# Three edits in the routed-expert tail of a fused vision kernel: when the experts' weights are asked for, what the token store waits for, and how 256 scatter slots are shared

## Chip, cores and metric

The kernel runs on one core of a Trainium2 chip. The metric is the device time of one execution in microseconds (us); of several runs the median counts. Five engines matter: TensorE (PE; its weight loads are shown as PEld), VectorE (DVE), ScalarE (ACT), GpSimd (POOL) and SyncE (SP), which only issues DMA transfers. ACT and POOL issue transfers as well. All of them run on the core's 16 DMA engines.

## The reference, cut to what matters

The input is `x` of shape (2, 64, 256, 256). Two blocks follow each other: a shift convolution with a recurrent layer over the 65,536 tokens, then a linear attention with a mixture of experts. The change touches only the last part, the experts. With 2 batches, 64 channels, 32 experts, 8 tokens for each expert and 256 hidden units it is:

```
probs = softmax(logits, axis=1)                      # over the tokens, for each expert
vals, idx = top_k(probs.transpose(0, 2, 1), K)       # 8 best tokens of each expert
gathered = take_along_axis(x, flat_idx[:, :, None], axis=1)
pooled = einsum('bked,bke->bed', gathered, topv)
h = gelu(einsum('ebd,edh->ebh', [pooled, 1], weight1))
out = einsum('ebh,eho->ebo', [h, 1], weight2)
outputs = zeros.at[batch, flat_idx].add(out * topv)  # scattered back to the tokens
x = x + outputs
```

So each batch has 32 x 8 = 256 slots, a slot being one (expert, token) pair. A token that several experts chose appears in several slots.

## The kernel before

Both batches lie beside each other on the 128 partitions, 64 channels each. The kernel is a series of blocks of engine programs. All up to the last stream the 65,536 tokens through the engines in tiles of 512 tokens and blocks of 2048, software-pipelined by an order written out by hand; that part is not touched. By its end each of 32 blocks of tokens has left its 8 best logits for each expert (`cand`), their places (`best_at`) and its sums of exponentials (`ses`), and the output without the experts' part is already in `out`.

The last block, the tail, is one serial program in which the engines wait for each other by semaphores. DVE counts its instructions on the semaphore `dv`; the names `DV_MAX`, `DV_TOK` and so on are the counts at which others may go on. In order:

1. SP merges the candidates of both halves with six transfers into `c2`, `i2`, `se2` (L1689 to L1691). ACT meanwhile asks for the experts' weights (L1711 to L1716), about 4.2 MB, loads a table (L1717) and then waits for `DV_MAX`.
2. DVE takes the maximum (`t8`, L1833), its places, and in eight steps the token numbers `tokf`, cast to `toki` (L1842). ACT takes two exponentials (L1719, L1720), and DVE scales them to the probabilities `prob` (L1847). That is `DV_TOK`.
3. SP stores `toki`, `tokf` and `prob` to DRAM (L1693 to L1695), waits for all three, and reads them back in the layouts that are needed: `toki2` (one slot for each partition, 4-byte pieces) on the semaphore `back`; `tokc` (likewise), and as broadcasts to all partitions `tokr`, `tokq`, `pr`, on `back2` (L1697 to L1703). The trace calls `toki2` token_of_slot and `tokq` token_by_channel.
4. From `toki2` DVE makes row addresses (L1855 to L1860), and POOL gathers the chosen tokens from DRAM with eight indirect transfers (L1744). DVE waits for all seven transfers of `back2` and finds which slots hold the same token (L1866, L1867), PE counts the later repeats (L1766), and DVE makes the scatter's addresses `word` and `byte_of_slot` (L1871 to L1875); all but the last slot of a token get an address past the end, and the transfer is skipped.
5. PE turns the gathered tokens (L1771), DVE copies them to `xg` (L1878), and the norm follows in short steps on PE, ACT and DVE; DVE multiplies by `pr` (L1882) and pools (L1883). PE waits for `w_loaded` and runs the experts: L1787 and L1790 with `w1` (64 weight loads of 128 columns), L1794 and L1798 with `w2` (128 of 64 columns). More short steps give `fin` (L1903), the new value of each slot's token.
6. `DV_FIN` releases the scatter. Slots 72 to 255 (`SHARED` = 184) are written by SP for the first batch and by ACT for the second, one transfer of 64 words for each slot, its address read from `byte_of_slot` into a register (L1676 to L1680). Slots 0 to 71 are written by POOL with one indirect transfer for both batches (L1751).

Of the kernel before, what the change touches and what calls it, by code (L numbers as in the profile page):

```python
# [7 lines left out]
F32 = mybir.dt.float32  # L8
# [3 lines left out]
ACT = mybir.ActivationFunctionType  # L12
# [3 lines left out]
B, C, H, W = 2, 64, 256, 256  # L16
P = B * C
# [11 lines left out]
E, K, HID = 32, 8, 256  # L29
# [38 lines left out]
def build_program(nc, x, conv_k, ffn_w, ffn_v, gamma, beta, q_w, q_b, kv_w, kv_b, proj_w, proj_b,  # L68
                  gate_w, gate_b, w1, w2, const, out, debug=None):
# [3 lines left out]
    with stack:  # L73
        def sb(name, shape, dt=F32, where=stack):
            return where.enter_context(nc.sbuf_tensor(name, shape, dt))
# [14 lines left out]
        tokf_d = dram("token_f_scratch", (B * E * K,))  # L90
        prob_d = dram("prob_scratch", (B * E * K,))
# [41 lines left out]
        with ExitStack() as ph:  # L133
# [7 lines left out]
            @blk.gpsimd  # L141
            def _(pool):
                for t in (w_rows, src["v"], src["q"], src["p"], src["g"], src["kv0"], src["kv1"]):
                    pool.memset(t[:, :], 0.0).then_inc(zeroed, 1)
                pool.memset(eps_c, EPS_C).then_inc(zeroed, 1)
                pool.memset(eps_t, EPS_T).then_inc(zeroed, 1)
                pool.memset(eps_z, EPS_Z).then_inc(zeroed, 1)
                pool.memset(ones[:, :], 1.0).then_inc(zeroed, 1)
                pool.memset(pair_mean[:, :], 0.0).then_inc(zeroed, 1)
                for b in range(B):  # L150
                    d = slice(b * C, (b + 1) * C)
                    for col, vec in ((qb, q_b), (pb, proj_b), (gam, gamma), (bet, beta)):
                        pool.dma_start(col[d, :], vec.rearrange("(c o) -> c o", o=1)).then_inc(vectors_loaded, 16)
                for r in range(4):
                    pool.dma_start(gb[r * E:(r + 1) * E, :], gate_b.rearrange("(c o) -> c o", o=1)).then_inc(vectors_loaded, 16)
# [62 lines left out]
        with ExitStack() as ph:  # L218
# [24 lines left out]
            S = lambda n: sem(n, ph)  # L243
# [416 lines left out]
        with ExitStack() as ph:  # L660
# [14 lines left out]
            S = lambda n: sem(n, ph)  # L675
# [262 lines left out]
        with ExitStack() as ph:  # L938
# [4 lines left out]
            S = lambda n: sem(n, ph)  # L943
# [87 lines left out]
        with ExitStack() as ph:  # L1031
# [15 lines left out]
            S = lambda n: sem(n, ph)  # L1047
# [543 lines left out]
        with ExitStack() as ph:  # L1591
            NC = NBLK * K
            w1_sb = sb("w1_sb", [P, E // 2, HID], F32, ph)
            w1b_sb = sb("w1b_sb", [E, HID], F32, ph)
            w2_sb = sb("w2_sb", [P, 2, E, C], F32, ph)
            w2b_sb = sb("w2b_sb", [E, C], F32, ph)
            cidx = sb("cidx", [P, NC], F32, ph)
            c2 = sb("c2", [64, 2 * NC], F32, ph)
# [53 lines left out]
            gp = S("tail_pool")  # L1652
            w_loaded = S("expert_weights_loaded")
            scat0, scat1 = S("columns_out_batch0"), S("columns_out_batch1")
            back2, rep, turned_back = S("broadcasts_back"), S("repeats_counted"), S("tokens_turned")
            blk = ph.enter_context(nc.Block())
            ONE = dict(allow_slow_non_contiguous=True)

            SHARED = 184
            AT_ONCE = 8
            SKIP = float(2 ** 28)
            PAST_END = float(4 * B * C * N)
# [18 lines left out]
            @blk.sync  # L1683
            def _(sp):

                sp.wait_ge(placed, 1)
                for j in range(2):
                    rows = slice(j * 64, (j + 1) * 64)
                    sp.dma_start(c2[:, j * NC:(j + 1) * NC], cand[rows, :]).then_inc(merged, 16)  # L1689
                    sp.dma_start(i2[:, j * NC:(j + 1) * NC], cidx[rows, :]).then_inc(merged, 16)  # L1690
                    sp.dma_start(se2[:, j * NBLK:(j + 1) * NBLK], ses[rows, :]).then_inc(merged, 16)  # L1691
                sp.wait_ge(dv, DV_TOK)
                sp.dma_start(tok_d.rearrange("(p k) -> p k", k=K), toki[:, :]).then_inc(out_tok, 16)  # L1693
                sp.dma_start(tokf_d.rearrange("(p k) -> p k", k=K), tokf[:, :]).then_inc(out_tok, 16)
                sp.dma_start(prob_d.rearrange("(p k) -> p k", k=K), prob[:, :]).then_inc(out_tok, 16)  # L1695
                sp.wait_ge(out_tok, 48)
                sp.dma_start(toki2[:, :, :].rearrange("p b j -> p (b j)"), tok_d.rearrange("(n p) -> p n", p=P), **ONE).then_inc(back, 16)  # L1697
                sp.dma_start(tokc[:, :, :].rearrange("p b j -> p (b j)"), tokf_d.rearrange("(n p) -> p n", p=P), **ONE).then_inc(back2, 16)
                for b in range(B):
                    rows = slice(b * C, (b + 1) * C)  # L1700
                    sp.dma_start(tokr[:, b, :], tokf_d[b * NS:(b + 1) * NS].partition_broadcast(P)).then_inc(back2, 16)
                    sp.dma_start(tokq[rows, :], tokf_d[b * NS:(b + 1) * NS].partition_broadcast(C)).then_inc(back2, 16)
                    sp.dma_start(pr[rows, :], prob_d[b * NS:(b + 1) * NS].partition_broadcast(C)).then_inc(back2, 16)  # L1703
                sp.wait_ge(back2, 16 * 7)
                sp.wait_ge(dv, DV_FIN)
                scatter(sp, 0, scat0)

            @blk.scalar
            def _(act):
                for j in range(2):  # L1710
                    act.dma_start(w1_sb[j * C:(j + 1) * C, :, :],  # L1711
                                  w1[j::2, 0:C, :].rearrange("e d h -> d e h")).then_inc(w_loaded, 16)
                act.dma_start(w1b_sb[:, :], w1[:, C, :]).then_inc(w_loaded, 16)  # L1713
                for j in range(2):
                    act.dma_start(w2_sb[:, j, :, :], w2[:, j * P:(j + 1) * P, :].rearrange("e p o -> p e o")).then_inc(w_loaded, 16)  # L1715
                act.dma_start(w2b_sb[:, :], w2[:, HID, :]).then_inc(w_loaded, 16)  # L1716
                act.preload_act_table_set("natural_log_exp_and_others")  # L1717
                act.wait_ge(dv, DV_MAX)
                act.activation(ex[:, :], c2[:, ::K], ACT.Exp, bias=nmx[:, 0:1]).then_inc(ac, 1)  # L1719
                act.activation(prob[:, :], t8[:, :], ACT.Exp, bias=nmx[:, 0:1]).then_inc(ac, 1)  # L1720
                act.wait_ge(mm, 1)
                act.activation(sqg[:, :], pgn[:, :], ACT.Square).then_inc(ac, 1)
                act.wait_ge(mm, 2)
                act.activation(lng[:, :], pgv[:, :], ACT.Ln, bias=eps_t).then_inc(ac, 1)
                act.wait_ge(ac, 4)
                act.activation(lng[:, :], lng[:, :], ACT.Exp, scale=-0.5).then_inc(ac, 1)
                act.preload_act_table(ACT.Gelu)
                act.wait_ge(mm, 4)
                act.activation(h1[:, :, :, :].rearrange("p j e b -> p (j e b)"),
                               ph1[:, :, :, :].rearrange("p j e b -> p (j e b)"), ACT.Gelu).then_inc(ac, 1)  # L1730
                act.wait_ge(dv, DV_FIN)
                scatter(act, 1, scat1)
# [27 lines left out]
            def _(pe):  # L1760
# [19 lines left out]
                m.then_inc(mm, 1)  # L1780
                pe.wait_ge(dv, DV_HIN)
                pe.wait_ge(gp, 1)
                pe.wait_ge(w_loaded, 16 * 6)

                each_twice = ident[0:E, 0:E].unsqueeze(2).to_broadcast([E, E, B])
                for j in range(2):
                    pe.matmul(ph1[:, j, :, :], w1b_sb[:, j * P:(j + 1) * P], each_twice, start=True,  # L1787
                              stop=False, skip_group_check=True)
                    for i in range(E // 2):
                        m = pe.matmul(ph1[:, j, 2 * i:2 * i + 2, :], w1_sb[:, i, j * P:(j + 1) * P], hin[:, i, :, :],  # L1790
                                      start=False, stop=True, skip_group_check=True)
                m.then_inc(mm, 1)
                pe.wait_ge(ac, 6)
# [1 line left out]
                          stop=False, skip_group_check=True)  # L1795
                for e in range(E):
                    for j in range(2):
                        m = pe.matmul(po[:, e, :], w2_sb[:, j, e, :], h1[:, j, e, :], start=False,  # L1798
                                      stop=(j == 1), skip_group_check=True)
                m.then_inc(mm, 1)  # L1800
                pe.wait_ge(dv, DV_OUT)
# [15 lines left out]
            def _(dve):  # L1817
                did = n_dv

                def go(ins):  # L1820

                    did[0] += 1
                    ins.then_inc(dv, 1)
                    dve.wait_ge(dv, did[0])
# [13 lines left out]
                for k in range(K):  # L1838
                    go(dve.scalar_tensor_tensor(out=jk[:, :], in0=iota_c[0:64, :], scalar=a8f[:, k:k + 1],
                                                in1=i2[:, :], op0=ALU.is_equal, op1=ALU.mult,  # L1840
                                                accum_out=tokf[:, k:k + 1]))
                go(dve.tensor_copy(toki[:, :], tokf[:, :]))  # L1842
                dve.wait_ge(ac, 2)
                go(dve.scalar_tensor_tensor(out=jk[:, 0:2 * NBLK], in0=ex[:, :], scalar=1.0, in1=se2[:, :],
                                            op0=ALU.mult, op1=ALU.mult, accum_out=nmx[:, 1:2]))
# [14 lines left out]
                        go(dve.tensor_scalar(row_at[:, h, b, :], row0[:, b, :], float((2 * b + h) * BLOCK), None, ALU.add))  # L1860
                assert did[0] == DV_ROWS

                dve.wait_ge(back2, 16 * 7)
                for b in range(B):
                    for j in range(2):
                        go(dve.tensor_scalar(eqm[:, b, j, :], tokr[:, b, :], tokc[:, b, j:j + 1], None, ALU.is_equal))  # L1866
# [12 lines left out]
                assert did[0] == DV_XG  # L1879
                dve.wait_ge(ac, 5)  # L1880
                go(dve.tensor_tensor(xgn[:, :], pgn[:, :], lng[:, :], ALU.mult))
                go(dve.tensor_tensor(xgn[:, :], xgn[:, :], pr[:, :], ALU.mult))  # L1882
                go(dve.tensor_reduce(pool_sb[:, :], xgn[:, :].rearrange("p (e k) -> p e k", k=K), AX.X, ALU.add))  # L1883
                assert did[0] == DV_POOL
# [21 lines left out]


DV_MAX = 6
DV_TOK = DV_MAX + 2 + K + 1 + 3
DV_ROWS = DV_TOK + 3 + 2 + 4  # L1910
DV_EQ = DV_ROWS + 2 * 4
DV_XG = DV_EQ + 4 + 1
# [27 lines left out]
```

## Time and profile before

| what | value |
|---|---|
| time, median of 3 runs | 1922.44 us (1921.51 to 1926.3) |
| the profiled execution's own time | 1924.74 us |
| its span, first to last instruction | 1922.9 us |
| busy shares of the span: PE, DVE, ACT, POOL | 81%, 75%, 64%, 75% |
| the tail, from about 1701 us to the end | some 222 us |
| scatter, from 1786.7 us to the end | some 136 us |

The span is what the profile shows between the first and the last instruction of the profiled execution; its own time has a little more around it. Busy shares are means over stages with different limits. In the tail the engines are mostly idle, so its rows are read one by one, in order of time, all from the start of the span. DMA-issuing instructions are shown on an engine's queue (SPq, ACTq) and are not counted as busy.

### The profile page before, as it was taken

The page shows a single profiled execution, that of the slowest core. Times are in us where ns is not written, and L with a number is a line of the kernel's source. Part 1 is how long each engine was busy: PE and PEld are TensorE (multiplying, and loading weights), DVE is VectorE, ACT ScalarE, POOL GpSimd, SP SyncE. Part 2 cuts the span into 40 slices and gives each one's busy share as a digit, 9 for nine tenths or more (in the row PEclk, how much of TensorE's full clock was granted, in tenths as well). Part 3 has the DMA queues.
Part 4 walks back from the last instruction along what each step waited for, and adds up shares of the span by engine and source line. Part 5 has one row for each costly group of instructions (what it writes and reads, how often), then busy time and mean ns, then how long its engine had stood idle before and what let it go on. Part 6 is the DMA issues. An engine that isn't in the chain of part 4 may idle for free. (4 is left out here: it accounts for less than half of the span.)

```text
span 1922.9 us, 24399 instructions
## 1 busy us (share of the span) xinstructions
PE 1556.5 (81%) x5627; PEld 648.4 (34%) x5627; DVE 1435.2 (75%) x2312; ACT 1238.3 (64%) x2178; POOL 1450.8 (75%) x1070
## 2 busy tenths in 40 slices
PE   4899999999999993698886679999999999816100
PEld 1333333333333331365553333333333333206000
DVE  1689999999999985498887547999999999951000
ACT  2777777777777751487875458889888888610000
POOL 2999999999999991058787129999999999901670
PEclk8999999999999996799988779999999999955555
DMA  4578888887888664989996527888888887570111
GB/s 152 163 230 254 251 234 256 251 254 234 253 254 252 192 192 152 313 278 373 368 391 269 219 45 209 287 287 287 285 284 275 278 286 246 192 179 13 2 2 1
DMA packets 114478, 429.81 MB, mean 224 GB/s; under 512 B 46720, under 2 KB 51744, under 8 KB 69280
## 3 DMA queue, kind: packets, MB, share of 16 engines
q1 hardware_dynamic: 92656, 423.78, 69.1%
q10 hardware_dynamic: 18736, 4.29, 1.5%
q8 instruction: 49, 0.80, 0.2%
q0 software_dynamic: 2944, 0.18, 0.1%
q14 instruction: 93, 0.76, 0.1%
HBM read 257.89 MB, written 170.01 MB: 223 GB/s over the span
## 5 line engine op out<-in xcount | busy, mean ns | idle before, releaser
L454 ACT ACTIVATE tap_products<-xn,kk 128x512 f32<-128x512 f32 x384 | 275.0, 718 | 156.6 <-POOL x_and_products L485 149.4
L485 POOL TENSOR_TENSOR x_and_products<-tap_products,x_and_products 128x512 f32<-128x512 f32 x256 | 327.1, 1278 | 41.5 <-POOL x_and_products L485 3.5
L385 PE MATMUL pst<-xn,taps 128*128 128x512 f32 x768 | 351.2, 592 | 0.0
L913 DVE SCALAR_TENSOR_TENSOR pss<-region,bn,pss 128x256 f32<-128x256 f32 x432 | 196.3, 489 | 67.4 <-PE pss L807 64.8
L1495 POOL TENSOR_SCALAR exp_q<-exp_q 128x512 f32<-128x512 f32 x128 | 189.3, 1479 | 73.3 <-ACT exp_q L1446 73.3
L852 POOL TENSOR_TENSOR x_block<-x_block,region 128x2048 f32<-128x2048 f32 x28 | 155.3, 5545 | 110.8 <-ACT region L839 88.5
L543 DVE SCALAR_TENSOR_TENSOR pst<-xn,kk,pst 128x512 f32<-128x512 f32 x256 | 192.2, 751 | 60.4 <-PE pst L385 60.2
L385 PEld LDWEIGHTS pst<-xn,taps 128*128 128x128 f32 x768 | 145.3, 189 | 186.3 <-issue 186.1
L1490 POOL TENSOR_TENSOR sq_norm<-x_ring 128x512 f32<-128x512 f32 x128 | 188.6, 1473 | 5.6 <-DVE x_ring L1542 1.7
L485 POOL TENSOR_TENSOR x_and_products<-tap_products,x_ring 128x512 f32<-128x512 f32 x128 | 163.4, 1277 | 19.2 <-ACT tap_products L454 19.2
L425 ACT ACTIVATE sq<-x_ring 128x512 f32<-128x512 f32 x256 | 157.6, 622 | 16.7 <-POOL x_ring L492 10.1
L1502 POOL TENSOR_TENSOR q_z<-q_map,z_inv 128x512 f32<-128x512 f32 x128 | 163.9, 1281 | 0.0
L492 POOL TENSOR_TENSOR x_ring<-acc,x_and_products 128x512 f32<-128x512 f32 x128 | 163.3, 1276 | 0.0
L807 PE MATMUL pss<-region,vT 128*128 128x256 f32 x480 | 137.5, 411 | 18.4 <-ACT region L839 18.2
L568 DVE TENSOR_TENSOR wx<-psw,rstd_wide 128x512 f32<-128x512 f32 x128 | 137.4, 1073 | 17.1 <-DMA rstd_wide<-rstd_scratch 10.9
L1379 PE MATMUL ps_denominator<-q_map,dT 128*128 128x512 f32 x256 | 138.5, 623 | 9.7 <-DVE q_map L1536 8.4
L1373 PE MATMUL ps_query<-x_ring,qcT 128*128 128x512 f32 x256 | 140.4, 632 | 4.0 <-DVE query L1527 4.0
L394 PE MATMUL psc<-x_ring,cst 128*128 128x512 f32 x256 | 140.1, 630 | 3.4 <-DVE xn L520 3.4
L400 PE MATMUL psw<-x_ring,wcT 128*128 128x512 f32 x256 | 132.9, 603 | 11.6 <-DVE wx L568 11.6
L807 PE MATMUL pss<-warm_state,vT 128*128 128x256 f32 x352 | 108.5, 431 | 40.2 <-ACT warm_state L839 22.1
L839 ACT ACTIVATE region<-pss,bn 128x256 f32<-128x256 f32 x256 | 116.6, 474 | 29.4 <-DVE pss L913 28.7
L1452 ACT ACTIVATE ln_d<-ps_denominator,cols 128x512 f32<-128x512 f32 x128 | 86.8, 678 | 73.2 <-PE ps_denominator L1379 73.0
(246 smaller groups left out, 2954.1 us busy)
## 6 DMA issues: line engine op xcount, KB each, us to landing
rstd_wide<-rstd_scratch SPq DMA_DIRECT2D x128, 512.0 KB, 7.2
x_ring<-in_x SPq DMA_DIRECT2D x32, 1024.0 KB, 5.3
x_scratch<-x_ring SPq DMA_DIRECT2D x32, 1024.0 KB, 4.3
xl_scratch<-wx SPq DMA_DIRECT2D x32, 1024.0 KB, 8.7
region<-xl_scratch SPq DMA_DIRECT2D x32, 1024.0 KB, 11.4
x_ring<-x_scratch SPq DMA_DIRECT2D x32, 1024.0 KB, 5.3
rstd_of_channels<-rstd_scratch SPq DMA_DIRECT2D x64, 512.0 KB, 7.5
out<-x_ring SPq DMA_DIRECT2D x32, 1024.0 KB, 6.6
```

The lines of the kernel that those rows point to most:

```text
L385: m = pe.matmul(wide(pst[g % 2]), taps[:, n * P:(n + 1) * P], tap_rows(g, t), start=(n == 0), stop=(n == len(PE_TAPS) - 1))
L425: act.activation(sq[l][:, g % TPB, :], x_tile(g), ACT.Square).then_inc(squared[l], 1)
L454: act.activation(prod[:, n, :, :], tap_rows(g, t), ACT.Copy, scale=kk[:, t:t + 1]).then_inc(products, 1)
L485: pool.tensor_tensor(xr[:, g % XR, :], prod[:, n, :, :].rearrange("p r w -> p (r w)"), xr[:, g % XR, :] if n else x_tile(g), ALU.add).then ...
L492: pool.tensor_tensor(x_tile(g), acc[:, g % 2, :, :].rearrange("p r w -> p (r w)"), xr[:, g % XR, :], ALU.add).then_inc(x1_ready, 1)
L543: dve.scalar_tensor_tensor(out=out, in0=tap_rows(g, t), scalar=kk[:, t:t + 1], in1=wide(pst[g % 2]), op0=ALU.mult, op1=ALU.add).then_inc(a ...
L807: pe.matmul(ps_at(r, j), vT[:, :], before, start=True, stop=True).then_inc(carried, 1)
L852: pool.tensor_tensor(in_chunks(x1_x2), in_chunks(x1_x2), y, ALU.add).then_inc(added, 1)
L913: dve.scalar_tensor_tensor(out=ps_at(r, j), in0=u, scalar=gain_w, in1=ps_at(r, j), op0=ALU.mult, op1=ALU.add).then_inc(summed, 1)
L1490: pool.tensor_tensor(sq[1][:, g % SQSLOTS[1], :], x_tile(g), x_tile(g), ALU.mult).then_inc(squared[1], 1)
L1495: pool.tensor_scalar(e, e, 1.0, None, ALU.min).then_inc(clipped, 1)
L1502: pool.tensor_tensor(qz[:, g % 2, :], qm[:, g % QSLOTS, :], zr[:, g % 2, :], ALU.mult).then_inc(qz_ready, 1)
```

## The change

- ACT first loads its table and takes both exponentials; only then does it ask for the weights.
- `w2` is laid out as pairs of hidden rows, so that each piece of its transfers is 512 bytes long and not 256: hidden unit 2p + j is on partition p. For this `w1` and its bias row are read by PE with a step of two columns. `w2`'s two transfers are now cut by experts, and `w2b` is asked for ahead of them.
- SP stores `toki` and `tokf` as soon as they are there (`DV_TOKI`), each on its own semaphore, reads `toki2` back after `toki` alone and the others after `tokf`; `prob` is stored after that, and the two `pr` broadcasts signal on `back`. DVE waits for `pr` only at L1882.
- `SHARED` is 168: SP and ACT scatter slots 88 to 255, POOL slots 0 to 87.

```
-            w2_sb = sb("w2_sb", [P, 2, E, C], F32, ph)
+            w2_sb = sb("w2_sb", [P, E, 2, C], F32, ph)
+            W2_PARTS = 2
...
-            SHARED = 184
+            SHARED = 168
...
-                sp.wait_ge(dv, DV_TOK)
+                sp.wait_ge(dv, DV_TOKI)
                 sp.dma_start(tok_d..., toki[:, :]).then_inc(out_tok, 16)
-                sp.dma_start(tokf_d..., tokf[:, :]).then_inc(out_tok, 16)
-                sp.dma_start(prob_d..., prob[:, :]).then_inc(out_tok, 16)
-                sp.wait_ge(out_tok, 48)
+                sp.dma_start(tokf_d..., tokf[:, :]).then_inc(out_tokf, 16)
+                sp.wait_ge(out_tok, 16)
                 sp.dma_start(toki2..., tok_d...).then_inc(back, 16)
+                sp.wait_ge(out_tokf, 16)
                 sp.dma_start(tokc..., tokf_d...).then_inc(back2, 16)
                 for b in range(B):
                     sp.dma_start(tokr[:, b, :], ...).then_inc(back2, 16)
                     sp.dma_start(tokq[rows, :], ...).then_inc(back2, 16)
-                    sp.dma_start(pr[rows, :], ...).then_inc(back2, 16)
-                sp.wait_ge(back2, 16 * 7)
+                sp.wait_ge(dv, DV_TOK)
+                sp.dma_start(prob_d..., prob[:, :]).then_inc(out_tokf, 16)
+                sp.wait_ge(out_tokf, 32)
+                sp.wait_ge(back, 16)
+                for b in range(B):
+                    sp.dma_start(pr[b * C:(b + 1) * C, :], ...).then_inc(back, 16)
+                sp.wait_ge(back2, 16 * 5)
+                sp.wait_ge(back, 16 * 3)
...
             def _(act):
+                act.preload_act_table_set("natural_log_exp_and_others")
+                act.wait_ge(dv, DV_MAX)
+                act.activation(ex[:, :], c2[:, ::K], ACT.Exp, ...).then_inc(ac, 1)
+                act.activation(prob[:, :], t8[:, :], ACT.Exp, ...).then_inc(ac, 1)
                 for j in range(2):
                     act.dma_start(w1_sb..., w1[j::2, 0:C, :]...).then_inc(w_loaded, 16)
                 act.dma_start(w1b_sb[:, :], w1[:, C, :]).then_inc(w_loaded, 16)
-                for j in range(2):
-                    act.dma_start(w2_sb[:, j, :, :], w2[:, j * P:(j + 1) * P, :].rearrange("e p o -> p e o")).then_inc(w_loaded, 16)
                 act.dma_start(w2b_sb[:, :], w2[:, HID, :]).then_inc(w_loaded, 16)
-                act.preload_act_table_set("natural_log_exp_and_others")
-                act.wait_ge(dv, DV_MAX)
-                act.activation(ex[:, :], ...)
-                act.activation(prob[:, :], ...)
+                for part in range(W2_PARTS):
+                    e = slice(part * E // W2_PARTS, (part + 1) * E // W2_PARTS)
+                    act.dma_start(w2_sb[:, e, :, :].rearrange("p e j o -> p e (j o)"),
+                                  w2[e, 0:HID, :].rearrange("e (p j) o -> p e (j o)", j=2)).then_inc(w_loaded, 16)
...
-                    pe.matmul(ph1[:, j, :, :], w1b_sb[:, j * P:(j + 1) * P], each_twice, ...)
+                    pe.matmul(ph1[:, j, :, :], w1b_sb[:, j::2], each_twice, ...)
                     for i in range(E // 2):
-                        m = pe.matmul(ph1[...], w1_sb[:, i, j * P:(j + 1) * P], hin[:, i, :, :], ...)
+                        m = pe.matmul(ph1[...], w1_sb[:, i, j::2], hin[:, i, :, :], ...)
...
-                dve.wait_ge(back2, 16 * 7)
+                dve.wait_ge(back2, 16 * 5)
...
+                dve.wait_ge(back, 16 * 3)
                 go(dve.tensor_tensor(xgn[:, :], xgn[:, :], pr[:, :], ALU.mult))
...
+DV_TOKI = DV_MAX + 2 + K + 1
+DV_TOK = DV_TOKI + 3
```

## Rows read from the trace of the kernel before

**Rows 1.** The page, chain that ended last: shares of the span by engine

```profile
POOL 4%; PE 2%; issue 2%; ACTq 1%; DMA 0%; DVE 0%; ACT 0%; POOLq 0%; SPq 0%; DVEq 0%
```

**Rows 2.** Timeline of the scatter: start, us, engine and line, operation, tiles, count

```profile
1786.73 1.02 POOL L1751 DMA_INDIRECT out<-fin,word_of_slot  x1 [45.13 <-DVE fin L1903]
1786.77 132.94 SPq L1679 DMA_DIRECT2D out<-fin  x184
1786.82 134.52 ACTq L1679 DMA_DIRECT2D out<-fin  x184
...
1878.16 0.98 POOL L1751 DMA_INDIRECT out<-fin,word_of_slot  x1 [0.30 <-issue]
```

**Rows 3.** Waits of SP's queue: line, waited for, us, times, longest

```profile
SPq L1591 <- DMA out<-fin: 1.2, 1, 1.2
```

**Rows 4.** Timeline, ACT's issues of 1860 to 1880 and of 1880 to 1900

```profile
1860.02 20.11 ACTq L1679 DMA_DIRECT2D out<-fin  x28
...
1879.63 20.35 ACTq L1679 DMA_DIRECT2D out<-fin  x28
```

**Rows 5.** Timeline of the tail's first part

```profile
1701.03 1.50 ACTq L1711 DMA_DIRECT2D w_sb<-in_L_ffn_weight  x2
...
1703.02 0.51 SPq L1689 DMA_DIRECT2D c<-cand  x1
...
1706.02 10.81 ACTq L1715 DMA_DIRECT2D w_sb<-in_L_ffn_weight  x1
1706.51 0.60 SPq L1691 DMA_DIRECT2D se<-ses  x1
1714.37 0.69 DVE L1833 MAX8 t<-c 64x8 f32<-64x512 f32 x1 [11.38 <-DMA se<-ses]
...
1722.56 0.16 DVE L1842 CAST toki<-tokf 64x8 int32<-64x8 f32 x1
1722.92 0.41 ACT L1719 ACTIVATE ex<-c,nmx 64x64 f32<-64x64 f32 x1
```

**Rows 6.** Packets, MB, share of 16 engines: 1702 to 1709, 1709 to 1714, 1714 to 1724

```profile
DMA packets 1224, 1.24 MB, mean 177 GB/s; under 512 B 16, under 2 KB 1224, under 8 KB 1224
q10 hardware_dynamic: 1224, 1.24, 94.1%
...
q10 hardware_dynamic: 973, 0.97, 87.3%
q1 hardware_dynamic: 480, 0.28, 26.8%
...
q10 hardware_dynamic: 2059, 2.03, 104.9%
```

**Rows 7.** DMA issues of 1700 to 1745: count, KB, median us from issue to landing

```profile
tokr<-token_f_scratch SPq DMA_DIRECT2D x2, 128.0 KB, 3.7
...
x_of_slot<-x_transposed,row_at POOLq DMA_INDIRECT x8, 2.4
...
token_scratch<-toki SPq DMA_DIRECT2D x1, 2.0 KB, 1.7
...
token_of_slot<-token_scratch SPq DMA_DIRECT2D x1, 2.0 KB, 2.1
```

**Rows 8.** Timeline from the token store to the first comparison of slots

```profile
1724.33 0.47 SPq L1693 DMA_DIRECT2D token_scratch<-toki  x1
...
1727.30 0.39 SPq L1697 DMA_DIRECT2D token_of_slot<-token_scratch  x1
...
1729.51 0.58 DVE L1855 TENSOR_SCALAR row_terms<-token_of_slot 128x4 int32<-128x4 int32 x3 [5.21 <-DMA token_of_slot<-token_scratch]
...
1734.62 0.35 DVE L1866 TENSOR_SCALAR eqm<-tokr,tokc 128x256 f32<-128x256 f32 x1 [3.32 <-DMA pr<-prob_scratch]
```

**Rows 9.** Timeline, the copy of the gathered tokens, with DVE's idle time before it

```profile
1743.90 0.42 DVE L1878 COPY xg<-pgv 128x256 f32<-128x256 f32 x1 [1.52 <-PE pgv L1771]
```

**Rows 10.** Timeline, ACT's square and the first half of the weight loads

```profile
1745.64 0.38 ACT L1722 ACTIVATE sqg<-pgn 128x256 f32<-128x256 f32 x1 [22.12 <-PE pgn L1774]
...
1751.55 6.90 PEld L1790 LDWEIGHTS ph<-hin,w_sb 128*128 128x128 f32 x32
```

## What I predict, and why

> **What bounds the kernel now.** I read the page first, and from its slices only that its last eighth is another kind of program: four engines run together up to about 1700 us, then almost nothing is busy. The diff touches only that tail, so the rest stays as it is. The chain of waits over the tail names POOL's scatter most [rows 1], and here the reader must be careful: SP's and ACT's DMA issues count as no work, so the chain ends on the last busy instruction, not on the last event. The timeline puts it right. Three engines scatter side by side: SP issues 184 transfers in 132.94 us, ACT 184 in 134.52 us, ending at 1921.34, and POOL 72 indirect ones, the last starting at 1878.16 and ending at 1879.14 [rows 2]. ACT's issue therefore sets the end, 1.2 us of landing follow [rows 3], and POOL stands idle for 42 us. Ahead of that is a serial chain from 1701 to 1787 us in which every step waits for one step of another engine.
>
> **Scatter.** One slot costs ACT 134.52/184 = 0.731 us and SP 0.722 us; one slot costs POOL (1878.16 - 1786.73)/71 = 1.288 us [rows 2]. The change moves 16 slots. ACT: 168 x 0.731 = 122.8, so 11.7 us less. SP: 121.4. POOL: 88 x 1.288 = 113.3 us, and with the 2.4 us in which an indirect transfer lands [rows 7] 116, some 7 us before ACT; it does not become the bound. Does a busier POOL slow the two issuers? With POOL at work ACT issued 28 in 20.11 us, with POOL done 28 in 20.35 us [rows 4]: no. A skipped repeat among the 16 moved slots could make them cheaper than the mean (bound below 11.0); the mean is my value, 11.7.
>
> **Front, first half: the merge.** ACT asks for the first weights at 1701.03, and SP's six small transfers (c, i, se) are issued from 1703.02 to 1707.11. The first DVE instruction that needs them starts at 1714.37, 7.9 us after the last was asked for [rows 5]. Small transfers with nothing in their way land in 1.7 to 3.7 us [rows 7]. The queue rows say where the rest goes: from 1702 to 1709 all 1224 packets are ACT's; only from 1709 to 1714 do SP's 480 run beside 973 of ACT's [rows 6]. With the weights asked for only after both exponentials, the last transfers (one of 64 KB, then the last se, asked for at 1706.51) should be there at 1708.4 to 1709.2, so MAX8 starts 5.2 to 6.0 us earlier; I take 5.6. From MAX8 to the end of toki's cast it is 1722.72 - 1714.37 = 8.35 us of DVE alone [rows 5]: toki is ready at 1717.1.
>
> Today toki then waits for the probabilities too. ACT was held by its own issue (10.81 us for one transfer) up to about 1721.6, its exponential starts at 1722.92 [rows 5], and the store of toki at 1724.33 [rows 8]. The table load moves to 1701, where ACT is idle, the exponentials to about 1709.7, and the store waits for toki alone: 1724.33 - 1717.1 = 7.2 us earlier. It is also waited for alone: it lands in 1.7 us [rows 7], while the read-back today is issued 1727.30 - 1724.33 = 2.97 us later because it waits for all three stores [rows 8]. That is 1.2 us more: 8.4 if nothing is in the way.
>
> **Front, second half: what is now in the way.** Both exponentials end near 1710.2, and there ACT starts to ask for the weights. Before, the weights' packets ran from 1702.5 to about 1723.9, 21.4 us [rows 6]; moved behind, they run from about 1712 to 1733. The store and every read-back of tokens lie inside that stretch, where before they had the DMA engines to themselves. In the mixed stretch the engines did 1453 packets in 5 us, 290 per us [rows 6]. By the code's shapes the token transfers are 512 packets of 4 bytes each for token_of_slot and tokc, then 384 of 1 KB for tokr and token_by_channel. If each has a packet of weights behind it, token_of_slot takes 512/290 = 1.8 us more than its 2.1 [rows 7] and lands 3.9 us after its issue; for the store I take 0.9 more than its 1.7 (its place in the queue is unknown). So toki goes out at 1717.1, is back at 1717.1 + 2.6 + 3.9 = 1723.6, and the row addresses and gathers start 5.9 us before today's 1729.51 [rows 8]. The other branch, tokc and the broadcasts: 2 x 1408/290 = 9.7 us from 1720.5 on, landed near 1730.7, against 1734.62 today (where two pr broadcasts are waited for as well): 3.9 us earlier. Today DVE is done with this second branch at 1742.38 and then idles 1.52 us until the gathered rows have come and are turned (xg at 1743.90) [rows 9]; that idle time is swallowed first, so by this branch xg starts 3.9 + 1.5 = 5.4 us earlier, by the first one 5.9. I take 5.0, a little less, since both branches queue on the same engines. The waits added in SP's queue hold up only the store of prob and the two pr broadcasts; asked for near 1725 and landed by 1734 to 1736 with the rest of the weights, they are first needed at L1882, 1748.8 today and some 1744 after, so 8 us of the gathers and of TensorE's and ACT's steps hide them. Without that cover each us of theirs would be one of the end.
>
> Here a row and a page differ. The Trainium skill (DMA: Bandwidth & Descriptors, section Queues, rings and completion order) says that each DMA engine takes turns between queues, one packet at a time; by that c would have started at once. The row of 1702 to 1709, with no packet of SP's, does not agree, and by the rule taken to its end the change would be worth 8.4 us in front and not 5.0.
>
> **Weights.** They are needed by PE at L1787, at 1751 today and at 1746 after; they arrive by 1733 to 1735, 11 us before. So their larger pieces are worth nothing here, fast or slow. ACT is next needed at L1722 (1745.64 today [rows 10], 1740.6 after); its issue, some 20.6 us long today, ends by 1731. If that cover were gone, each us late would be a us of the end.
>
> **Strided weight loads.** L1790 and L1787 now read every second column. 32 loads take 6.90 us today [rows 10], 0.216 us each, 64 of them on the path: 13.8 us. No strided weight load is in the trace. Lower bound nothing. The nearest row for a stepped read is far: ACT read 64 values in steps of eight in 0.41 us [rows 5] and 256 adjacent ones in 0.38 us [rows 10], at most 4.3 times as much per value. Spread evenly over the steps that is 1 + 3.3/7 = 1.5 times for a step of two, 6.5 us; with the whole factor it is 13.8 x 3.3 = 45.5 us. I take 0, since a step of two is nearer to adjacent reads than to a step of eight and the 4.3 leaves out whatever part of ACT's 0.41 us is fixed, and keep 6.5 for the range.
>
> The Trainium skill (SBUF — State Buffer, section Door 1: The DMA port swizzle) puts lines of 16 bytes behind this and lets fp32 step by up to four for free, which the stepped ACT row does not contradict, being beyond four. By it the price is 0.
>
> **Sum.** Scatter -11.7, front -5.0, strides 0: -16.7. The profiled execution took 1924.74 us (span 1922.9 and 1.8 around it): 1908.0. It was 2.3 above the median of the runs, 1922.44, and so the median after should be 1905.7.
>
> **Rivals.**
> Free DMA engines, as by the page's rule: the token transfers slip between the weights without loss. For it: the small transfers moved freely once they had begun (480 packets within 5 us). Front -8.4: 1922.4 - 11.7 - 8.4 = 1902.3. Chance 0.15.
> Weights in the way: each big transfer of ACT holds SP's back until it is almost handed out, as it did from 1703 to 1709. For it: that very row; against it: when the store comes (6.6 us after the first weights are asked for) the hold of 1703 to 1709 would just be over. If it repeats with each piece, the broadcasts are held to about 1731.7 and land 3.7 us later, at 1735.4, 0.8 after today's 1734.62. DVE's idle 1.5 us takes that up, the front gives nothing and only the scatter counts: 1910.7. Chance 0.23.
> The strides cost a little (1.5 times, +6.5): 1912.2. Chance 0.06.
> The other side: the strides cost the full 4.3 times, +45.5: 1951. It decides from 16.7 + 5.8 = 22.5 us on, a weight load of 0.216 + 22.5/64 = 0.57 us in place of 0.216. For it only the ACT row; against it that this row steps four times as far. Chance 0.04.
> The rest, 0.52, is the forecast, with its own range of 1903.5 to 1908.5.
>
> **Numbers.** Range 1901.8 to 1912.8: it holds the forecast, both DMA rivals and the small stride price. That is more than 8 in 10 by my chances, but some of it is lost to the spread from run to run (1921.51 to 1926.3). A change under 0.3% (5.8 us) could not be told from none. Faster by more than that means under 1916.7: all cases but the large stride and unforeseen ones, 0.90; within 0.06; slower 0.04.
>
> **What would show it.** Scatter: 168 issues each on SP and ACT in 121 to 123 us, 88 on POOL in 113, ACT last. Merge: MAX8 within 6.5 us of SP's first issue (now 11.3). Order: the store of toki right after the cast, no wait for ACT. Second half: the time from toki's store to DVE's first row_terms, 5.2 us now, 6 to 7 by the forecast, over 9 if weights are in the way, 4 if the engines are free; and from that store to the first eqm, 10.3 us now, 13.6 by the forecast. Strides: 32 loads at L1790 in 6.9 us. The prediction is wrong if the weights land after 1747, if ACT is still issuing at 1741, if POOL ends last, or if the weight loads lengthen.

## The result, and the profile after

The changed kernel took 1914.14 us (median of 6 runs, 1909.63 to 1917.6), the kernel before beside it 1924.22 (6 runs, 1921.51 to 1926.48). The ratio is 0.9944, with a 95% interval of 0.993 to 0.9959: faster by 0.56%, some 10.8 us. I had forecast 16.7 us less and a range of 1901.8 to 1912.8; the median lies 1.3 us above it. The kernel before ran 1.8 us slower in this set than in the runs on which I had built the forecast (1924.22 against 1922.44), so the gain is the better measure: 10.8 us in place of 16.7. The direction was right, the size was not.

The profiled execution has a span of 1912.9 us, 10.0 less than before. Its tail, in order of time:

```profile
1703.46 0.51 SPq L1691 DMA_DIRECT2D c<-cand  x1
...
1708.39 0.69 DVE L1844 MAX8 t<-c 64x8 f32<-64x512 f32 x1 [4.95 <-DMA se<-ses]
...
1709.29 0.79 ACTq L1724 DMA_DIRECT2D w_sb<-in_L_ffn_weight  x1
...
1714.79 8.00 ACTq L1730 DMA_DIRECT2D w_sb<-in_L_ffn_weight  x1
...
1716.57 0.16 DVE L1853 CAST toki<-tokf 64x8 int32<-64x8 f32 x1
1716.76 0.47 SPq L1695 DMA_DIRECT2D token_scratch<-toki  x1
...
1724.63 0.40 SPq L1698 DMA_DIRECT2D token_of_slot<-token_scratch  x1
...
1730.96 0.58 DVE L1867 TENSOR_SCALAR row_terms<-token_of_slot 128x4 int32<-128x4 int32 x3 [13.52 <-DMA token_of_slot<-token_scratch]
...
1732.78 0.35 DVE L1878 TENSOR_SCALAR eqm<-tokr,tokc 128x256 f32<-128x256 f32 x1
...
1745.28 0.42 DVE L1890 COPY xg<-pgv 128x256 f32<-128x256 f32 x1 [4.77 <-PE pgv L1782]
...
1752.93 6.90 PEld L1801 LDWEIGHTS ph<-hin,w_sb 128*128 128x128 f32 x32
```

Two things are to be seen. MAX8 starts 4.9 us after SP's first request, where it was 11.35 [rows 5]. And the token store, asked for at 1716.76, is followed by its read-back only at 1724.63, 7.9 us later (2.97 before [rows 8]), and that one by row_terms another 6.3 us later (2.2 before). What was gained by 1717 is gone by 1731. The landings say the same (count, KB, median us to landing, requests of 1700 to 1745):

```profile
tokr<-token_f_scratch SPq DMA_DIRECT2D x2, 128.0 KB, 4.8
...
se<-ses SPq DMA_DIRECT2D x2, 8.0 KB, 1.8
...
token_scratch<-toki SPq DMA_DIRECT2D x1, 2.0 KB, 7.9
...
token_of_slot<-token_scratch SPq DMA_DIRECT2D x1, 2.0 KB, 6.2
```

Before, the last se needed some 7.9 us, and the two token transfers 1.7 and 2.1 [rows 7]. The packets of each queue, first from 1717 to 1723 and then from 1723 to 1728:

```profile
DMA packets 1102, 1.27 MB, mean 212 GB/s; under 512 B 80, under 2 KB 890, under 8 KB 1102
...
q10 hardware_dynamic: 1102, 1.27, 112.6%
...
q10 hardware_dynamic: 728, 1.46, 104.2%
q1 hardware_dynamic: 160, 0.00, 2.3%
```

In the six microseconds after the request no packet of SP's queue (q1) moves, all 1102 are weights (q10). The first one moves at 1723.12, 6.4 us after the request, while weights still run (the last at 1729.45). It is the picture of rows 6 once more, with the token store in c's place.

The scatter in the timeline, with the last row from the waits of SP's queue:

```profile
1786.81 0.42 DVE L1916 TENSOR_TENSOR fin<-xg,pc 128x256 f32<-128x256 f32 x1 [2.16 <-PE pc L1823]
...
1788.16 121.39 SPq L1681 DMA_DIRECT2D out<-fin  x168
1788.20 123.11 ACTq L1681 DMA_DIRECT2D out<-fin  x168
...
1900.20 0.98 POOL L1762 DMA_INDIRECT out<-fin,word_of_slot  x1 [0.30 <-issue]
...
SPq L1591 <- DMA out<-fin: 1.3, 1, 1.3
```

ACT's issue is 11.4 us shorter than in rows 2 and still the last.

The start of the tail moves from one execution to the next (1694.5 to 1706.3 us in the profiles below), and nothing of the change is in that. So I count in the tail's own time, from POOL's first memset (1701.02 before, 1701.46 after), and give for each kernel, in us, where each step starts and how long it is from fin to the end of the span. (row_terms is DVE's first instruction on the tokens read back, xg its copy of the gathered tokens.) Changed to before: start +0.4, fin +0.9, from fin to the end -11.4, together -10.0.

| kernel | MAX8 | token store | row_terms | xg | fin | fin to end |
|---|---|---|---|---|---|---|
| before | 13.4 | 23.3 | 28.5 | 42.9 | 84.4 | 137.5 |
| changed | 6.9 | 15.3 | 29.5 | 43.8 | 85.4 | 126.1 |
| scatter alone | 13.3 | 22.9 | 28.1 | 42.6 | 84.1 | 125.9 |
| front alone | 6.9 | 15.3 | 29.3 | 43.7 | 85.2 | 136.8 |
| weights early | 13.4 | 21.8 | 25.7 | 40.0 | 81.6 | 125.4 |
| weights after the token | 6.9 | 15.3 | 19.2 | 39.1 | 80.6 | 126.1 |
| small pieces | 6.9 | 15.3 | 27.8 | 42.2 | 83.7 | 125.6 |
| weights by POOL | 6.9 | 15.5 | 29.8 | 44.2 | 85.8 | 124.7 |
| w2, then w1 | 6.9 | 15.3 | 21.5 | 43.1 | 84.7 | 125.9 |
| 164 slots | 6.9 | 15.3 | 29.3 | 43.6 | 85.2 | 129.3 |
| weights in the gaps | 6.9 | 15.3 | 19.2 | 33.6 | 75.1 | 125.9 |
| old store order | 6.9 | 16.0 | 29.1 | 43.7 | 85.2 | 124.7 |
| 160 slots | 6.9 | 15.3 | 29.4 | 43.7 | 85.3 | 134.7 |

The nine kernels with 168 slots have 124.7 to 126.1 us from fin to the end, so a difference of a microsecond there says nothing. Small pieces, weights by POOL, old store order and 160 slots were run once each (1917.42, 1907.03, 1911.56 and 1916.33 us); only their traces are read. The 1907.03 us are a tail that started early, at 1694.8, and not a shorter one.

### The profile page after: what moved, and what is told of

Same layout as the page of the kernel before. It is cut to its first block and busy times, and to the rows that moved or that the text cites. A ratio compares the mean times of both kernels' runs of the same rounds, so it can differ in the third digit from the quotient of the medians.

```text
span 1912.9 us, 24349 instructions
## 1 busy us (share of the span) xinstructions
PE 1553.3 (81%) x5627; PEld 645.6 (34%) x5627; DVE 1437.4 (75%) x2312; ACT 1238.2 (65%) x2178; POOL 1466.9 (77%) x1086
## 5 line engine op out<-in xcount | busy, mean ns | idle before, releaser
L425 ACT ACTIVATE sq<-x_ring 128x512 f32<-128x512 f32 x256 | 157.6, 622 | 17.1 <-POOL x_ring L492 10.1
L807 PE MATMUL pss<-region,vT 128*128 128x256 f32 x480 | 136.3, 408 | 19.2 <-ACT region L839 19.1
L400 PE MATMUL psw<-x_ring,wcT 128*128 128x512 f32 x256 | 132.7, 603 | 11.6 <-DVE wx L568 11.6
L1762 POOL DMA_INDIRECT out<-fin,word_of_slot x88 | 86.5, 983 | 71.6 <-DVE fin L1916 45.1
L807 PE MATMUL pss<-warm_state,vT 128*128 128x256 f32 x352 | 105.3, 419 | 43.7 <-ACT warm_state L839 25.5
## 6 DMA issues: line engine op xcount, KB each, us to landing
region<-xl_scratch SPq DMA_DIRECT2D x32, 1024.0 KB, 11.4
```

The source lines that it names most:

```text
L425: act.activation(sq[l][:, g % TPB, :], x_tile(g), ACT.Square).then_inc(squared[l], 1)
L807: pe.matmul(ps_at(r, j), vT[:, :], before, start=True, stop=True).then_inc(carried, 1)
L1762: pool.indirect_dma_start(out=out_words, out_offset=bass.IndirectOffsetOnAxis(ap=word[:, s:s + 1], axis=0), in_=fin[:, s:s + 1], in_offset ...
```

## The experiments

The store and its read-back were held. The theory to be tested, called H at first and then D: a transfer's packets start only when what the other queues have already handed to the DMA engines is done. Its rivals: P, the queues only share the engines, as I had reckoned; T, a request waits for whole transfers of the other queue; G, SP and ACT share the unit that makes the descriptors, and the wait is there.

### Each half alone

```
-            SHARED = 184          # in the kernel before
+            SHARED = 168
```

> The kernel before with SHARED = 168 alone. If the whole gain of the changed kernel is the scatter, this is 11.7 us faster than before (16 slots at 0.731 us), as fast as or a little faster than the changed kernel. If the front gave part of the gain, it is slower than the changed kernel. ACT's 168 issues take 122.8 us, POOL's 88 take 113.

Ratio to before 0.9948 (0.9931 to 0.9966), in one set with the next three. 0.52% of that set's median of before, 1926.43 us, is 10.0 us; the trace has 11.6 us less from fin to the end (137.5 to 125.9). The changed kernel's gain is the scatter's.

```
-            SHARED = 168          # in the changed kernel
+            SHARED = 184
```

> The changed kernel with SHARED = 184, so only its front. Theory H (a request of SP waits until ACT's requests that were taken before it are handed out to the DMA engines): the merge gives 6 us, the held store and read-back of tokens take them back, sum 0 to +1 us against before. Rival P (packets of the two queues only share the DMA engines): 3 to 5 us faster than before, as I had predicted, and the trace of the changed kernel was a rare case.

Ratio 1.0009 (0.9998 to 1.002), fin at 85.2 against 84.4. The front gave nothing, and the store landed after 7.8 us here too. P, by which the front alone would have gained 3 to 5 us, falls.

### When the weights are asked for

```
 def _(act):                                 # in the changed kernel
+    (w1, w1b, w2b, w2 asked for here)
     act.preload_act_table_set(...)
     (wait for DV_MAX, both exponentials)
-    (w1, w1b, w2b, w2 asked for here)
```

> The changed kernel with the weights asked for first, as before, ahead of the table load and the exponentials; everything else stays. By H: the merge is held again (MAX8 6 us later, at 1714.4), but the token store goes out at 1722.8 onto free DMA engines, lands in 1.7 us and its read-back in 2.1 us; row_terms starts at about 1726.8 in place of 1731.0, so some 4 us faster than the changed kernel. If the later weights were worth something in themselves (P), it is slower than the changed kernel by the merge's 6 us less what sharing costs.

Ratio 0.9929 (0.9907 to 0.9951). MAX8 is back at 13.4, but the store and read-back are free (1.7 and 2.1 us) and row_terms comes 3.8 us before the changed kernel's, xg too:

```profile
1725.69 0.47 SPq L1695 DMA_DIRECT2D token_scratch<-toki  x1
1727.38 0.40 SPq L1698 DMA_DIRECT2D token_of_slot<-token_scratch  x1
1729.60 0.58 DVE L1867 TENSOR_SCALAR row_terms<-token_of_slot 128x4 int32<-128x4 int32 x3 [3.22 <-DMA token_of_slot<-token_scratch]
```

The scatter alone has the weights in the same early place and the old order of the stores, and its fin is at 84.1 against 81.6 here. So where the token transfers find the way free, the new order is worth up to 2.5 us; w2's pieces differ too, and no run parts the two. And with the new order the old place of the weights is the better one: one hold of 6 us for the merge costs less than two in a row for the tokens. By the timed ratios alone this kernel (0.9929) and the changed one (0.9944, from another set) are not told apart; the trace does it, by 3.8 us at fin.

```
     (both exponentials)                     # in the changed kernel
+    act.wait_ge(back, 16)
     (w1, w1b, w2b, w2 asked for here)
```

> The changed kernel, and ACT asks for the weights only when token_of_slot is back. Both the merge and the token store have the DMA engines to themselves: row_terms near 1720.8, and if nothing else is late xg some 8 us earlier than in the changed kernel. By H the store of prob, issued behind the broadcasts, is now held by w1 and pr may come late for L1895 (needed near 1742), which would take 0 to 3 us back; the weights run from about 1722 to 1741, just ahead of PE's need near 1744. Expected 5 to 8 us faster than the changed kernel. By P: 3 to 4 us faster, since sharing cost no more than that.

Ratio 0.9922 (0.9897 to 0.9947), fin 4.8 us earlier than in the changed kernel; I had expected 5 to 8. row_terms came at 19.2, 10.3 us earlier, but then it was the gathers' turn, which I had not seen coming. The packets from 1724 to 1730, then from 1730 to 1733, and the landing of the gathers:

```profile
q10 hardware_dynamic: 1061, 1.08, 84.9%
q1 hardware_dynamic: 249, 0.17, 14.1%
...
q10 hardware_dynamic: 540, 0.55, 105.8%
q0 software_dynamic: 64, 0.03, 7.6%
...
x_of_slot<-x_transposed,row_at POOLq DMA_INDIRECT x8, 8.8
```

POOL's first gather is asked for at 1723.39. Its queue, q0, has no packet before 1730, and a gather lands after 8.8 us in place of 2.4 [rows 7]. The hold is not SP's alone.

### What holds: transfers, descriptors or the DMA engines

```
     for j in range(2):                      # in the changed kernel
+        for q in range(4):                  # w1 in 8 transfers of 256 KB
...
-            W2_PARTS = 2
+            W2_PARTS = 8
```

> The changed kernel with w1 asked for in 8 transfers and w2 in 8, in place of 2 and 2, in the same place and order. Theory D (a request starts only when the packets that other queues had handed to the DMA engines before it are done, about 1024 of them, 64 for each engine, whatever transfers they belong to): the token store still lands 7 to 8 us after its issue. Rival T (a request waits for the end of whole transfers of the other queue): the pieces are a quarter as long, so the store lands after 3 to 4 us. In both the weights take about as long.

The store landed after 7.5 us and not after 3 to 4; T falls. From 1722 to 1727 only weights moved, and in this kernel they were 1253 packets:

```profile
q10 hardware_dynamic: 1253, 0.99, 115.6%
...
token_scratch<-toki SPq DMA_DIRECT2D x1, 2.0 KB, 7.5
```

The same transfers from POOL's queue:

```
 def _(act):                                 # in the changed kernel
-    (w1, w1b, w2b, w2 asked for here)
 def _(pool):
     (memsets)
+    pool.wait_ge(dv, DV_MAX)
+    (w1, w1b, w2b, w2 asked for here)
```

> The changed kernel with the same weight transfers asked for by POOL on its own queue after DV_MAX, in place of ACT. Rival G (SP and ACT share the unit that makes the descriptors, and that is what holds SP): POOL's queue isn't part of it, the token store lands in 1.7 to 3 us. Theory D (the packets already handed to the DMA engines hold it): it lands late again, 5 to 8 us. POOL may be busy with making the descriptors and come late to the gathers, so the time itself tells little.

It landed after 8.5 us; G falls. From 1711 to 1716, after the store's request at 1710.31, with not one packet of SP's:

```profile
DMA packets 309, 0.98 MB, mean 196 GB/s; under 512 B 48, under 2 KB 64, under 8 KB 309
...
q0 software_dynamic: 309, 0.98, 104.6%
...
token_scratch<-toki SPq DMA_DIRECT2D x1, 2.0 KB, 8.5
```

So the hold does not depend on which queue asked, nor on the size of the transfers. In packets it is 309 or 1253 in five microseconds, so it is not a number of packets as the trace counts them, as I had written in the expectation. Taken from the store's request to the first packet of SP's queue, bytes and time are alike: 1.37 MB in 6.4 us in the changed kernel, 1.36 MB in 6.4 us with small pieces, 1.38 MB in 6.6 us by POOL. Whether it is a number of bytes or a time, no run here separates, and none shows where between the queues and the memory a request waits.

The Trainium skill (DMA: Bandwidth & Descriptors, section Issuing engines are not separate DMA queues) says that transfers from SP, ACT and GpSimd end up on the same 16 DMA engines, whoever starts them. The last experiment agrees: the store is held behind either queue, 8.5 us behind POOL's, 7.9 behind ACT's. That the wait is in the DMA engines themselves is not shown.

### Weights where nobody waits

```
     (both exponentials)                     # in the changed kernel
+    (w1b, w2b, w2 asked for here, on a semaphore of their own)
+    act.wait_ge(dv, DV_EQ + 1)
+    (w1 asked for here)
```

> The changed kernel with the weights in two groups on two semaphores: w1's bias row and all of w2 right behind the exponentials, w1 only when DVE has counted the repeats (DV_EQ + 1), near the last gather. By D: w2 is 1024 packets of 2 KB and is through about 1717, when the token store goes out at 1717; store and read-back take 2 to 3 us each, row_terms at 1721 to 1723, the gathers land unhindered, xg near 1736, w1 arrives at 1743 to 1745 and PE waits some 1 to 2 us for it. 6 to 8 us faster than the changed kernel, 17 to 19 faster than before. If the waits were not the cause, it is as fast as the changed kernel.

A miss: ratio 0.9942 (0.9927 to 0.9958), fin only 0.7 us before the changed kernel's. The store landed in 4.0 us, since w2 was not quite through, and row_terms came at 21.5. But w1 was asked for just ahead of the last of the eight gathers, and that one alone was held:

```profile
1736.49 1.40 ACTq L1731 DMA_DIRECT2D w_sb<-in_L_ffn_weight  x2
1737.40 0.94 POOL L1756 DMA_INDIRECT x_of_slot<-x_transposed,row_at  x1 [0.31 <-issue]
...
1747.92 0.42 DVE L1892 COPY xg<-pgv 128x256 f32<-128x256 f32 x1 [10.03 <-PE pgv L1783]
```

DVE's idle time before xg is 10.0 us. This gather landed 9.7 us after its request, where one landed in 2.4 [rows 7]: w1 was asked for 0.9 us too early, and it cost over seven.

```
     (both exponentials)                     # in the changed kernel
+    (half of w1, w1b)
+    act.wait_ge(dv, DV_EQ + 4)
+    (other half of w1)
     (square, ln, exp of the norm)
+    (w2b, w2, on a semaphore of their own)
```

> The changed kernel with the weights put where nobody else asks the DMA engines for anything: half of w1 and its bias row behind the exponentials (1 MB, through before the token store goes out), the other half when byte_of_slot is made (DV_EQ + 4, behind the last gather's request), w2 behind the norm's last exponential. By theory D nothing of SP or POOL waits: counted from the tail's start the token store at 15.3, its read-back asked for at 17.0, row_terms at 19.2, xg near 34.5 (43.8 in the changed kernel), fin near 76 (85.35 in the changed kernel, 84.41 before). About 9 us faster than the changed kernel, 20 faster than before. If D is wrong, store or gathers land late all the same and xg stays above 39.

Ratio to before 0.9887 (0.9871 to 0.9902): 1904.34 us against 1926.55, the fastest kernel of this study. fin is at 75.1, as expected, 10.2 us before the changed kernel's. Everything lands as if alone:

```profile
1724.83 0.58 DVE L1870 TENSOR_SCALAR row_terms<-token_of_slot 128x4 int32<-128x4 int32 x3 [3.21 <-DMA token_of_slot<-token_scratch]
...
1736.17 0.94 POOL L1757 DMA_INDIRECT x_of_slot<-x_transposed,row_at  x1 [0.30 <-issue]
1736.69 0.63 ACTq L1727 DMA_DIRECT2D w_sb<-in_L_ffn_weight  x1
...
1739.26 0.42 DVE L1893 COPY xg<-pgv 128x256 f32<-128x256 f32 x1 [2.60 <-PE pgv L1784]
```

The second half of w1 follows the last gather's request by 0.5 us, and PE starts the experts at 1746.29 without a wait for it.

```
     (SP's stores, read-backs and waits, DVE's waits)   # in the changed kernel
-    toki, tokf; read back; prob behind them
+    toki, tokf, prob; wait for all three; read back    # as before
```

> The changed kernel with the stores and read-backs in the old order and with the old waits (all three stores behind the probabilities, read-back behind all three). The stores are held by the weights all the same, so by D the new order is worth 1 to 2 us here and not the 1.2 + 1.6 us and more that free DMA engines would make of it: fin 1 to 2 us later than in the changed kernel, counted from the tail's start.

fin is at 85.2, no later than the changed kernel's 85.4: even the 1 to 2 us that I had left to the new order are not there. The store is asked for 0.7 us later and the read-back 1.8 us later, and then less of the weights is ahead of them: the store lands in 7.6 us, not 7.9, the read-back in 4.1, not 6.2. In the changed kernel the second edit buys nothing; where the weights are out of the way it can, as weights early showed.

### The division of the scatter

```
-            SHARED = 168                    # in the changed kernel
+            SHARED = 164
-            AT_ONCE = 8
+            AT_ONCE = 4
```

> The changed kernel with 164 slots on SP and ACT and 92 on POOL, address registers loaded four at a time (164 isn't a multiple of 8). At 0.731 and 1.288 us for a slot ACT ends after 119.9 and POOL after 118.5 us and its landing: 3 us faster than the changed kernel. If loading four at a time costs a slot more than before (twice as many loads), it is 0 to 2 us faster.

Ratio 0.996 (0.9947 to 0.9974), and from fin to the end it is 129.3 us, 3.2 more than with 168. ACT's issue was shorter (121.86 us) but not by 2.9: a slot cost 0.743 us. And something else set the end. SP waits at the block's end for another engine (the page names PE's sequencer, which has nothing left to do), in the kernel with 164 slots, then with 160:

```profile
SPq L1591 <- PEq L1591: 7.5, 1, 7.5
```

```profile
SPq L1591 <- PEq L1591: 16.3, 1, 16.3
```

```
-            SHARED = 168                    # in the changed kernel
+            SHARED = 160
```

> The changed kernel with 160 slots on SP and ACT, 96 on POOL. ACT's issue takes 117, POOL's 123.6 us. If POOL only had to wait for its landing, POOL would end some 6 us behind ACT's issue and the scatter would last about as long as in the changed kernel (123.6 + 1.3 + 1.2 against 123.1 + 1.5). Theory Q (behind its last transfer POOL needs another 8.3 us until the block's end, as the traces of the kernel with 164 slots and of the changed one let me read): the span ends 9 us after POOL's last landing, so 134 to 135 us from fin's end to the end of the span, some 9 us more than the changed kernel.

134.7 us from fin to the end, as theory Q had it, 8.6 more than with 168. POOL's last transfer is the row to read:

```profile
1903.42 0.98 POOL L1762 DMA_INDIRECT out<-fin,word_of_slot  x1 [0.31 <-issue]
```

It ends at 1904.40 and the span at 1914.54, 10.1 us later; with 164 slots it was 1905.35 and 1915.18, 9.8 us. What lies between is a DRAIN on POOL's own sequencer at the block's end. Its rows (ns, and the start in us), for the kernel before, the changed one, 164 and 160 slots:

```profile
L1591 POOLq DRAIN  x1: 6598/6598/6598, 1880.5 to 1880.5; - x1
L1591 POOLq DRAIN  x1: 7905/7905/7905, 1902.5 to 1902.5; - x1
L1591 POOLq DRAIN  x1: 8232/8232/8232, 1906.7 to 1906.7; - x1
L1591 POOLq DRAIN  x1: 8558/8558/8558, 1905.8 to 1905.8; - x1
```

With 72, 88, 92 and 96 slots on POOL it grows by 0.08 us for each, so a slot costs POOL 1.288 us of issue and 0.08 of this. With 164 and 160 slots the span ends 0.2 us after it. In the changed kernel it is over at 1910.4, and ACT is last, at 1912.92: POOL is only 2.2 us from setting the end, where I had reckoned 7. By these figures, as an estimate, one slot more for POOL (1.37 us) and one less for ACT (0.73) would all but use that up.

## Why the prediction was wrong

**Scatter**, forecast -11.7: right. ACT's issue went from 134.52 to 123.11, fin to the end from 137.5 to 126.1, -11.4. The scatter alone gave 11.6 by its trace. That POOL would be no bound was right, but by luck: I had counted 2.4 us of landing, and nothing for the 7.9 us of DRAIN at its end.

**Merge**, forecast -5.6: right, though a little small. MAX8 came 6.4 us earlier in the tail's time.

**Order of the stores**, forecast: the store asked for 7.2 us earlier. It was 8.0. This step was right as well.

**The step that failed** is "If each has a packet of weights behind it": from the mixed stretch of rows 6 I took a sharing of the engines, packet by packet, and gave the store 0.9 and the read-back 1.8 us more. They took 6.2 and 4.1 us more than when free (7.9 and 6.2 in place of 1.7 and 2.1). The front was forecast at -5.0 and came out at +0.9; that is 5.9 of the missing us, the scatter's 0.3 works the same way. The answer was in rows 6 itself: seven microseconds with no packet of SP's. I used it against the rule of turns between queues (the Trainium skill, DMA: Bandwidth & Descriptors, section Queues, rings and completion order), and then reckoned the second half by that very rule. What decided here is how much of other queues was asked for ahead of a request, not how the queues take turns after it.

**The rival "weights in the way"** (chance 0.23) had the mechanism and the time nearly right, 1910.7 against 1914.14, or 11.7 us of gain against 10.8. My argument against it, that the hold would just be over when the store came, was the error: I took the hold of rows 6 for that of the first transfer alone, over once it was through. But it falls on every request that comes while weights are still ahead: the store 7.5 us after the first weights were asked for, and after it the read-back. The mark I had set for it, over 9 us from the store to row_terms, was met with 14.2. The other branch, to eqm, took 16.0 us, not 13.6 (and by its own sum, 1720.5 + 9.7, I should have written 1730.2 for its landing, not 1730.7), and yet DVE idled 4.8 us before xg: the first branch, the one to the gathers, was the late one. So the rival's price came near by another path than its own.

Of the signs that I had called fatal none came: the weights landed by 1730.6, ACT had issued them by 1722.8, POOL did not end last, and the weight loads kept their length. They all watched whether somebody waits for the weights or for POOL, and none of them who waits behind the weights.

**Strides**, forecast 0: right. 32 loads take 6.90 us, as in rows 10. The Trainium skill (SBUF — State Buffer, section Door 1: The DMA port swizzle) had them free up to a step of four fp32 values; the trace agrees at a step of two.

**Larger pieces**: as forecast hidden, though they are not without effect. From 1723 to 1728, with w2 in pieces of 512 bytes, the weights moved at 292 GB/s (1.46 MB in 5 us), from 1714 to 1724 before, mostly w2 in pieces of 256 at 203 GB/s (2.03 MB in 10 us [rows 6]). No run changes the pieces alone, so that they are the cause is not shown. Nobody waited for the weights.

## What to carry to other kernels

A large transfer is not free because its data are needed late. Here it delayed the small requests that came within its time, of whatever queue, by 2 to 7 us (the store 2.3 and 6.2, the read-back 2.0 and 4.1, a gather 7.3). So ask for it in stretches in which nobody else asks for anything on the path, in lots that are through when the next request comes; here that turned a gain of 10.8 us (1924.22 to 1914.14, ratio 0.9944) into one of some 22 (1926.55 to 1904.34, ratio 0.9887). Look in a trace for a stretch in which a queue with open requests moves no packet, and ask of each edit that moves a bulk transfer whom it will now stand in front of. When work is divided between engines, measure each engine's end at the end of the block, not at its last transfer.

## What the runs showed of the hardware

- A request had no packet moved for 6.4 to 6.9 us while 1.3 to 1.4 MB of others went ahead: SP's store behind ACT's weights (changed kernel, 6.4 us, 1.37 MB), the same with transfers of a quarter of the size (6.4, 1.36), SP's store behind POOL's weights (6.6, 1.38), POOL's first gather when ACT's weights ran (weights after the token, 6.9, 1.37, 1.14 of it weights), SP's first c in the kernel before (6.6, 1.33). With the way free the store's first packet moved 1.1 us after its request.
- It was not a number of packets: those in front were 1178, 1899 and some 400 in the first three.
- At the end of the block POOL's sequencer had a DRAIN of 6.60, 7.90, 8.23 and 8.56 us with 72, 88, 92 and 96 indirect transfers of the scatter. In the two kernels in which POOL was last the span ended 9.8 and 10.1 us after its last transfer; behind ACT's last transfer it was 1.6 us (1911.31 to 1912.92).
